# Slot list spread over shared jobs, a one-hot product on GpSimd, results stored ahead of weight loads, routed jobs written out, and a reordered end in an attention and expert layer

## The reference, cut to what matters

```python
h = _layernorm(x) * (1 + cb) + sb
scores = softmax(h @ gate_weight.T)                 # 2048 rows, 8 experts
topk_w, topk_idx = top_k(scores, 2)
topk_w = topk_w / (sum(topk_w) + 1e-20)
cw = zeros((T, E)).at[arange(T)[:, None], topk_idx].add(topk_w)
g = silu(einsum('th,efh->tef', x, w_gate)) * einsum('th,efh->tef', x, w_up)    # F = 352
expert_out = einsum('tef,ehf->teh', g, w_down)
y = einsum('te,teh->th', cw, expert_out) + swiglu(x, shared weights of width 704)
x = x + gb * y
```

## Time and profile before

| what | value |
|---|---|
| median of 3 executions | 1620.08 us (1616.24, 1620.08, 1622.06) |
| profiled execution | 1621.21 us |
| its span in the trace | 1619.4 us |
| TensorE busy in the span | 1539.6 us, 95% |
| VectorE / ScalarE / GpSimd busy | 1026.9 / 727.8 / 667.8 us |
| mean granted TensorE clock | 0.98 |

### The profile page before, as it was taken

The page is one execution under the profiler, slowest core; times in us unless marked ns, Lnnn a source line. Parts: engine busy times, 40 slices in busy tenths (PEclk is TensorE's granted clock), DMA queues, the critical chain, the costliest instruction groups (busy, mean ns, idle before and its releaser), DMA issues.

```text
span 1619.4 us, 29774 instructions
## 1 busy us (share of the span) xinstructions
PE 1539.6 (95%) x8844; PEld 1364.3 (84%) x8845; DVE 1026.9 (63%) x2255; ACT 727.8 (45%) x1728; POOL 667.8 (41%) x713
## 2 busy tenths in 40 slices
PE   6899999997999999999999999979999899999997
PEld 3677778886999999999999999868988788888896
DVE  5966666665777777777777777876576222222267
ACT  3542222345666666666666666522231232233232
POOL 2113333345666665656666666525212111111053
PEclk9999999997999999999999999989998999999999
DMA  7335555576748475757665666274131455755465
GB/s 257 137 130 180 204 202 199 191 258 215 240 148 252 144 240 165 241 172 220 191 202 184 210 182 215 102 265 173 63 115 55 171 180 204 264 194 196 173 199 172
DMA packets 203231, 303.81 MB, mean 188 GB/s; under 512 B 80337, under 2 KB 142161, under 8 KB 196001
## 3 DMA queue, kind: packets, MB, share of 16 engines
q1 hardware_dynamic: 193312, 276.82, 50.7%
q0 software_dynamic: 5680, 18.62, 4.0%
q10 hardware_dynamic: 4176, 7.60, 1.4%
HBM read 187.35 MB, written 115.64 MB: 187 GB/s over the span
## 4 chain that ended last, share of the span: by engine, by line
PE 77%; DVE 9%; DMA 8%; issue 3%; ACT 2%; POOL 1%; SPq 0%; ACTq 0%; DVEq 0%; POOLq 0%
PE bank L1405 40%; PE bank L1500 15%; PE bank L1613 7%; PE bank L1565 7%; DMA slot_results<-y_sb 6%; PE bank L1596 4%; PE bank L1662 1%; PE bank L1418 1%; PE bank L1698 1%; DMA keys<-k_ring 1%; DVE ht_lo L2184 1%; DVE h L2162 1%; DVE h L2165 1%; DMA xin<-ffn_rows,slot_tokens 1%; ACT prob L1235 0%
## 5 line engine op out<-in xcount | busy, mean ns | idle before, releaser
L1405 PE MATMUL bank<-w,xt_hi 128*128 (+2 forms) x1136 | 286.3, 334 | 7.5 <-issue 4.6
L1405 PEld LDWEIGHTS bank<-w,xt_hi 128*128 128x128 f32 x1136 | 198.3, 191 | 19.4 <-issue 14.9
L1405 PE MATMUL bank<-w,xt_lo 128*128 (+2 forms) x568 | 185.3, 326 | 0.0
L1247 ACT ACTIVATE prob<-prob,row_inv 128x128 f32<-128x128 f32 (+3 forms) x256 | 137.2, 560 | 82.0 <-DVE row_inv L2056 81.8
L2184 DVE TENSOR_TENSOR ht_lo<-bank,ht_hi 128x128 fp32r<-128x128 f32 (+1 forms) x213 | 48.3, 282 | 195.1 <-ACT ht_hi L1342 194.9
L1405 PE MATMUL bank<-w,ht_hi 128*128 (+3 forms) x426 | 143.4, 418 | 23.3 <-DVE ht_lo L2184 23.3
L1235 ACT ACTIVATE prob<-bank,neg_max 128x128 f32<-128x128 f32 (+3 forms) x256 | 133.8, 526 | 49.0 <-DVE neg_max L2048 48.8
L1405 PE MATMUL bank<-wv_hi,h_hi 128*128 128x256 f32 x512 | 148.5, 290 | 0.0
L1405 PE MATMUL bank<-wv_lo,h_hi 128*128 128x256 f32 x512 | 145.7, 285 | 0.0
L1405 PE MATMUL bank<-wv_hi,h_lo 128*128 128x256 f32 x512 | 145.7, 285 | 0.0
L900 POOL CAST q_hi<-q_raw 128x512 fp32r<-128x512 f32 x64 | 71.5, 1118 | 137.7 <-PE bank L1565 117.1
(11 more groups left out here) (227 smaller groups left out, 4101.0 us busy)
## 6 DMA issues: line engine op xcount, KB each, us to landing
keys<-k_ring SPq DMA_DIRECT2D x64, 512.0 KB, 3.0
ch_raw<-wexp SPq DMA_DIRECT2D x128, 170.0 KB, 3.1
experts_hi<-ch_hi SPq DMA_DIRECT2D x128, 170.0 KB, 2.6
experts_lo<-ch_lo SPq DMA_DIRECT2D x128, 170.0 KB, 2.7
w<-experts_hi SPq DMA_DIRECT2D x10, 2176.0 KB, 8.9
w<-experts_lo SPq DMA_DIRECT2D x10, 2176.0 KB, 15.3
q_transposed<-q_out SPq DMA_DIRECT2D x64, 256.0 KB, 2.0
k_even<-keys SPq DMA_DIRECT2D x16, 1024.0 KB, 5.5
```

Of the source, the lines that this page charges most:

```text
L1247: ins = act.activation(part, part, ACT.Copy, scale=row_inv[:, h, r:r + 1])
L1405: ins = pe.matmul(dst, a, m, start=(k == 0), stop=(k == last))
```

## The change

- **Slot list.** The routing work of VectorE is dealt out differently: `slots_of` and both `position` calls run inside job 17, the one-hots of c = 0 inside job 18 and those of c = 1 inside job 19 (both `lanes` of a c together), the copy of the slot list and `begun` inside job 20, `halves` behind it, and `table` inside job 21. TensorE's two `slot_tokens` move from the ends of jobs 18 and 19 into jobs 19 and 20, between the up product and the transposes of the next rows.
- **A product on GpSimd.** `tile_hot` = `tile_eq` times `token` moves from VectorE to GpSimd, ahead of `add_shared(17)` and `add_shared(18)`.
- **GpSimd order.** `gather_x(2)` goes ahead of `add_shared(20)` and `add_shared(21)`, and for every later slot `gather_x(r + 1)` goes ahead of `weights_ready(r)`.
- **Stores first.** SyncE stores the result of slot r-1 ahead of the weight loads of step r, not behind them.
- **Routed jobs written out.** On TensorE all 39 slots stand one after the other without a loop, and the offset of the next slot is read once, ahead of `down`.
- **The end.** The last addition to `acc` of six tiles (`by_pool`: places 0, 2, 4, 6, 8, 10 of `GATHER`) moves from VectorE to GpSimd, which makes it ahead of the gathers that reuse the buffer. In the last job VectorE combines tile 15 and adds it to `acc` ahead of the last `ht_part`, then finishes tile 14 while TensorE makes the last product, and then adds the last bank times `gb` to tile 15.

```diff
--- before
+++ after
@@ -74,7 +74,12 @@
-TOKENS_AT = [NT + 2, NT + 3]
+def by_pool(i):
+    return i % 2 == 0 and i < NT - TT
+TOKENS_AT = [NT + 3, NT + 4]
@@ -570,6 +575,11 @@
+        def finished(i):
+            return ((f_pool, i // 2 + 1) if by_pool(i) else
+                    (f_ok, len([k for k in range(i + 1) if not by_pool(k)])))
@@ -828,6 +838,8 @@
                 n = r + R0
                 nxt = sp.value_load(tab[0:1, 3, bass.ds(r, 1)], min_val=1, max_val=E + 1)
                 load = [sp.value_load(tab[0:1, 4 + s, bass.ds(r, 1)], min_val=0, max_val=1) for s in range(2)]
+                if not (isinstance(r, int) and r == 0):
+                    store_y(r - 1, (k + 1) % 2)
                 wait_apart(sp, (y_full, n))
@@ -835,8 +847,6 @@
                           .then_inc(w_ld[s], 16)
-                if not (isinstance(r, int) and r == 0):
-                    store_y(r - 1, (k + 1) % 2)
@@ -852,7 +862,7 @@
             for i, t in enumerate(GATHER):
-                sp.wait_ge(f_ok, i + 1)
+                sp.wait_ge(*finished(i))
                 sp.dma_start(out_t[:, t, :], acc[:, t, :]).then_inc(out_st, 16)
@@ -1042,8 +1052,16 @@
-            for n in range(NT + 1, NT + 3):
-                add_shared(n)
+            def tile_match(c):
+                pool.wait_ge(tile_eq_ok, c + 1)
+                pool.tensor_tensor(tile_hot[:, c, :, :], tile_eq[:, c, :, :],
+                                   cf("token", NT).unsqueeze(2).to_broadcast([P, NT, NOH]),
+                                   ALU.mult).then_inc(tile_hot_ok, 1)
+            for c in range(2):
+                tile_match(c)
+                add_shared(NT + 1 + c)
@@ -1073,20 +1091,29 @@
             weights_ready(1)
+            gather_x(2)
             add_shared(R0 - 2)
             add_shared(R0 - 1)
-            gather_x(2)
             for r in range(2, NSLOT):
-                weights_ready(r)
                 if r + 1 < NSLOT:
                     gather_x(r + 1)
+                weights_ready(r)
+            def add_tile(i):
+                pool.wait_ge(f_gb, i + 1)
+                a = acc[:, GATHER[i], :]
+                pool.tensor_tensor(a, a, h2[:, i % TT, :], ALU.add).then_inc(f_pool, 1)
...
                 if i >= TT:
-                    pool.wait_ge(f_ok, i - TT + 1)
+                    if by_pool(i - TT):
+                        add_tile(i - TT)
+                    pool.wait_ge(*finished(i - TT))
                 for c, rows in enumerate((xr, h2)):
@@ -1708,15 +1735,19 @@
             def job(n, s, wofs, prev_ofs, route=False, prev=True, nxt=True, free=None, up_ld=None, prev_at=WD,
-                    gathered=False):
+                    gathered=False, amid=None, ahead=None):
                 half(n, s, wofs, 0, route)
...
                 half(n, s, wofs, 1, route)
+                if amid:
+                    amid()
                 if nxt:
                     turn_rows(n + 1, 1 - s, loaded(n + 1, 1 - s, gathered))
+                if ahead:
+                    ahead()
                 if prev:
@@ -1758,9 +1789,8 @@
             for n in range(NT + 1, R0):
-                job(n, n % 2, W1, W1, free=(y_gb, n - 2))
-                if n in TOKENS_AT:
-                    slot_tokens(TOKENS_AT.index(n))
+                job(n, n % 2, W1, W1, free=(y_gb, n - 2),
+                    amid=(lambda: slot_tokens(TOKENS_AT.index(n))) if n in TOKENS_AT else None)
@@ -1770,30 +1800,19 @@
-            def routed(j):
-                for k in range(2):
-                    r = j * 2 + k
-                    n = r + R0
-                    if k == 1:
-                        was = at
-                    at = offset(r)
-                    if isinstance(j, int) and j == 0:
-                        prev_ofs, free = W1 if k == 0 else was, (y_gb, n - 2)
-                    else:
-                        prev_ofs = was if k == 1 else offset(r - 1)
-                        free = (y_gb, R0) if isinstance(j, int) and j == 1 and k == 0 else (y_ev, r - 2)
-                    pe.wait_ge(w_ready, r + 1)
-                    job(n, k, at, prev_ofs, free=free, gathered=True)
-            routed(0)
-            routed(1)
-            with pe.Fori(2, NSLOT // 2) as j:
-                routed(j)
-            r = NSLOT - 1
-            pe.wait_ge(w_ready, r + 1)
-            job(r + R0, 0, offset(r), offset(r - 1), free=(y_ev, r - 2))
+            at = [offset(0)]
+            def next_offset(r):
+                if r < NSLOT:
+                    at.append(offset(r))
+            for r in range(NSLOT):
+                n = r + R0
+                pe.wait_ge(w_ready, r + 1)
+                job(n, r % 2, at[r], at[r - 1] if r else W1, free=(y_gb, n - 2) if r < 3 else (y_ev, r - 2),
+                    gathered=r + 1 < NSLOT, ahead=lambda: next_offset(r + 1))
             pe.wait_ge(w_ld[0], 32 * (E // 2 + 1))
-            job(Z0, 1, 0, offset(r), free=(y_ev, NSLOT - 2))
+            job(Z0, 1, 0, at[NSLOT - 1], free=(y_ev, NSLOT - 2))
             for n in range(Z0 + 1, NJ):
@@ -2348,12 +2366,10 @@
-                link(dve.tensor_tensor(tile_eq[:, c, :, :],
-                                       cf("slot_tile", NOH).unsqueeze(1).to_broadcast([P, NT, NOH]),
-                                       pos_f[:, c, 1, :].unsqueeze(2).to_broadcast([P, NT, NOH]), ALU.is_equal))
-                dve.tensor_tensor(tile_hot[:, c, :, :], tile_eq[:, c, :, :],
-                                  cf("token", NT).unsqueeze(2).to_broadcast([P, NT, NOH]),
-                                  ALU.mult).then_inc(tile_hot_ok, 1)
+                dve.tensor_tensor(tile_eq[:, c, :, :],
+                                  cf("slot_tile", NOH).unsqueeze(1).to_broadcast([P, NT, NOH]),
+                                  pos_f[:, c, 1, :].unsqueeze(2).to_broadcast([P, NT, NOH]),
+                                  ALU.is_equal).then_inc(tile_eq_ok, 1)
@@ -2411,24 +2427,31 @@
             first_tiles()
-            shared_job(NT + 1, slots_of)
-            position(0)
-            position(1)
+            def positions():
+                slots_of()
+                position(0)
+                position(1)
+            def one_hots(c):
+                if c == 0:
+                    dve.wait_ge(x1_ok, B)
+                    dve.wait_ge(h2_st, 16 * B + 32)
+                tile_match(c)
+                lanes(c, 0)
+                lanes(c, 1)
+            def tokens():
+                slot_tokens()
+                begun()
+            shared_job(NT + 1, positions)
             parts(0)
             parts(1)
-            dve.wait_ge(x1_ok, B)
-            dve.wait_ge(h2_st, 16 * B + 32)
-            tile_match(0)
-            lanes(0, 0)
-            shared_job(NT + 2, lambda: lanes(0, 1))
-            tile_match(1)
-            lanes(1, 0)
-            shared_job(NT + 3, lambda: lanes(1, 1))
-            begun()
-            slot_tokens()
-            shared_job(NT + 4, halves)
-            table()
-            shared_job(NT + 5)
+            shared_job(NT + 2, lambda: one_hots(0))
+            shared_job(NT + 3, lambda: one_hots(1))
+            shared_job(NT + 4, tokens)
+            halves()
+            shared_job(NT + 5, table)
             weights()
@@ -2459,8 +2485,9 @@
                 dve.tensor_tensor(a, a, mods[:, t // TT, 3, :], ALU.mult).then_inc(f_gb, 1)
-                dve.wait_ge(f_gb, i + 1)
-                dve.tensor_tensor(acc[:, t, :], acc[:, t, :], a, ALU.add).then_inc(f_ok, 1)
+                if not by_pool(i):
+                    dve.wait_ge(f_gb, i + 1)
+                    dve.tensor_tensor(acc[:, t, :], acc[:, t, :], a, ALU.add).then_inc(f_ok, 1)
@@ -2468,18 +2495,24 @@
-            for n in range(Z0, NJ):
+            for n in range(Z0, NJ - 1):
                 k = n - Z0
-                job(n, n % 2, "routed", n + 1 < NJ)
+                job(n, n % 2, "routed", True)
                 if k >= 2:
                     both(2 * k - 4)
-                    if k == NB2 - 1:
-                        combine(2 * k - 3)
-                    else:
-                        both(2 * k - 3)
+                    both(2 * k - 3)
+            job(NJ - 1, (NJ - 1) % 2, "routed", False)
+            a, gb = h2[:, (NT - 1) % TT, :], mods[:, B - 1, 3, :]
+            combine(NT - 1)
+            link(dve.tensor_tensor(a, a, gb, ALU.mult))
+            link(dve.tensor_tensor(acc[:, NT - 1, :], acc[:, NT - 1, :], a, ALU.add))
             ht_part(NJ - 1)
-            add_last(NT - 1)
-            finish_tile(NT - 1)
+            both(NT - 2)
+            dve.wait_ge(y_full, NJ)
+            link(dve.tensor_tensor(a, bank[4 + (NJ - 1) % 2][:, :], gb, ALU.mult))
+            dve.tensor_tensor(acc[:, NT - 1, :], acc[:, NT - 1, :], a, ALU.add).then_inc(f_ok, 1)
```

More of the change, by code:

```diff
@@ L476, in adaln_layer @@
         c_stat = sem("c_stat")
-        g_hi_ok = sem("g_hi_ok")
         h2_ok = sem("h2_ok")
@@ L515, in adaln_layer @@
         f_w2 = sem("f_w2")
```

(10 more changed lines are left out.)

## The result

| | before | after |
|---|---|---|
| median | 1619.65 us (1616.24 to 1622.06, 4 executions) | 1592.15 us (1589.26 to 1593.91, 4 executions) |
| profiled execution | 1621.21 us | 1593.91 us |
| span | 1619.4 us | 1592.0 us |
| mean granted clock | 0.98 | 0.988 |

The ratio is 0.9827, with a 95% interval from 0.9806 to 0.9847: 27.5 us faster. I had predicted 1593.

What follows compares the result with a forecast made beforehand. TensorE, busy 95% of the span, was taken as the bound, leaving only gaps and lower-clock time to win. From 1621.2 us, -8.0 + 6.3 - 8.6 - 15.0 + 1.0 - 3.6 = -27.9 gave 1593.3, forecast 1593, range 1586 to 1604.

Steps and rivals of the forecast that it cites:

- Slot list, -8.0: Jobs 18 to 21: TensorE's 3.25 us gap for `ht_lo` shrinks to 0.4 and the lower clock goes, gaining 8.0 us.
- Product on GpSimd, at nothing: Job 18: the `tile_hot` product moved to GpSimd takes 1.6 us, waits for one `lane_hot`, and adds nothing to the sum.
- My bound of 2.2 for its duration: GpSimd's product was to take 1.6 to 2.2 us; at 2.2 it would be 0.1 late for `slot_tokens(0)`.
- Table, +6.3: Start of job 22: the later `table` delays `w_ready`, a new 4.1 us gap plus 2.2 for the clock, losing 6.3 us.
- The price of the clock, 2.2: Behind the new gap at the table: lower clock costs between 0 and 5.2 us, taken as 2.2.
- Gather, -8.6: Job 23 to 24: `gather_x(2)` issued before the weight load removes TensorE's 6.39 us wait and its clock loss, gaining 8.6 us.
- 0 to 1 us to spare: `gather_x(3)`, in the old place behind the load, just fits; if it doesn't, the gather gain is 7.6 us.
- Slots, -15.0: Jobs 24 to 58: stores first and jobs written out regain 15.0 of 15.4 us lost, bounds 4.5 and 15.4.
- the loop was not the cost: Rival on the slots: offsets and register addresses cost the same in straight code, 10.5 us stay, 1604 us; chance 0.12.
- Additions on GpSimd, +1.0: Last shared jobs: six additions leave VectorE, but GpSimd's SBUF additions slow its steps; a loss of 1.0 us, between -1.7 and +3.
- The end, -3.6: Last job: last product starts 2.0 us earlier and runs 1.5 shorter, later links save 0.1; gain 3.6, or 1.9 us.
- Ahead of 1200 us, at nothing: Before 1200 us: only one rewritten wait between two VectorE steps on the gate columns, costed at nothing.

Runs made afterwards that it cites:

- before, stores first: The kernel before with each result store moved ahead of the weight loads, slots still in a loop: median 1609.82 us, ratio to before 0.9931.
- before, slots written out: The kernel before with only TensorE's routed slots written out straight and the offset read once: median 1624.83 us, ratio to before 1.0016.

## Why the prediction was right, and where not

**Slot list, -8.0: right, 7.5.** The gap went as walked, to 0.64 and not to 0.4. A cast in `parts` took 1.16 us at 1217.13, where the other casts take 0.18, since it ran beside GpSimd's addition (1216.96 to 1218.25, where the cast ends at 1218.29). These 0.98 us are more than the whole gap of 0.64: without them I would expect none. No run undid this edit alone. Of the 7.5 us, 2.6 are the gap and 4.9 the clock behind it, and the latter is not fixed: in "before, stores first" the same gap cost 3.2 us less, and against that profile the edit would have been worth 4.3.

**Product on GpSimd, at nothing: right.** My bound of 2.2 for its duration was broken, by a mechanism that I had named for the additions and not carried over far enough. The first product took 3.32 us and began inside the pair of `lane_hot`: from the pair's end at 1223.68 to its own at 1224.81 are 1.1 us. The second took 2.18 us, and there one of the two `lane_hot` took 2.29 where the earlier trace rows has 1.22. So the product itself is an estimated 1.1 us, and it waits for one or two `lane_hot`, or they for it. TensorE came 1.3 us later still (1226.1), so the cover of a microsecond held.

**Table, +6.3: the gap right in kind, both sizes too large.** 3.02 for 4.1, of which 1.0 is the table itself: its nine steps took 2.0 us, while my 3.0 came from the earlier trace rows, in which one step had run beside GpSimd. The price of the clock, 2.2, was 0 in this execution and in four others with the same gap, and 1.5 and 2.5 in two. So 2.2 lies in the range and is too large on average, 0.6 over the seven. Of the 3.5 us, 0.5 lie in the two jobs beside the gap and are not named by any wait. So -1.1 in the gap, -2.2 in the clock and +0.5 make the -2.8 by which this term was over.

**Gather, -8.6: right to 0.1,** alone (15.34 to 6.72) and in the whole. `gather_x(3)` had "0 to 1 us to spare": 24 to 25 took 7.16, 0.4 more than 6.72, and in two later profiles of nine the gather was late and the step took 8.35 and 8.48.

**Slots, -15.0: the total right (14.6), the split wrong.** This is the step of the prediction that failed. I split 15.4 us into 4.5 for stores, 4.6 for turns and the rest, as shares that add, each read from TensorE's own list of waits. They don't add. Stores first alone gave 9.2, straight jobs alone nothing (a loss of 2.6 in the profile), the two together 15.1. A store that lands late holds ScalarE for up to 5.2 us, and the time that TensorE loses at its turns meanwhile makes its wait shorter; so what TensorE waits for by name, 4.5 us, was the part the turns didn't cover. I also left out that a longer wait can bring the lower clock, 1.3 to 1.6 us each time in the two straight kernels with late stores. My rival "the loop was not the cost" was not true either: with the stores out of the way the turns cost 5.9. The sum held because the change made both edits. Had only the straight code been changed, the same working would have promised 10 us for none. On this the Trainium skill's page "Runtime: NRT & Kernel Launch" (section "Instruction fetch mechanics") was right in that straight code cost nothing more, 6.72 us for each of 33 jobs. That a taken branch costs something fits the 0.35 us a turn, though the second offset read at the turn is in it too.

**Additions on GpSimd, +1.0: somewhat low, 1.9 in the marks, 1.7 to 2.2 by the experiment.** Beside GpSimd's 1.31 an addition of VectorE took 2.02, which is 0.69 + 1.31, so it waited for the whole of the other. The Trainium skill's page "SBUF — State Buffer" (section "Who interferes with whom") has this exclusion, and these rows agree. The 3.4 us that I worked out by it were too much; that TensorE's pace hid the rest was not tested. The edit was a small loss.

**The end, -3.6: right, 4.0,** and 3.6 by experiment. A product start 1.7 us earlier (3.35 to 1.64) and a product at the full clock, 2.34 us in place of 3.82, 1.5 us. I had 2.0 and 1.5, and 0.1 for the last links; 0.9 came ahead of and behind the product. VectorE's steps of tile 14 now end 0.4 us behind the product, so an even faster product would have given nothing.

**Ahead of 1200 us, at nothing: +1.9.** All of it lies ahead of job 1, whose mark stands at 1085.63 before and 1087.57 after; from there to job 16 both took 113.5 us. Nothing of the change lies there, and the stretch moves from execution to execution: in three profiles of after the mark stands at 1087.57, 1084.31 and 1081.08. The jobs from 1 to 16 took between 113.1 and 118.3 us over all the profiles as well. The sum had no term for any of this, and it happened to cancel against the table.

The forecast's 1593 therefore came out close in part by luck, because terms were off by up to 2.8 us in opposite directions. Measured less predicted, they are -2.8 at the table, +1.9 ahead of job 1, +0.9 at the additions, and about half a microsecond or less elsewhere. The median was to stand 1.1 us under the profiled execution, so the sum as written gives 1592.2, which I had put at 1593. The mechanisms of the other terms held; the largest term, the slots, had the right total and the wrong working.

## What to carry to other kernels

- A wait that TensorE's list names is only what is left after its other delays have covered the rest. Before splitting a loss into shares, ask which delay hides which. The pair that interacts should be tried alone, both ways.
- Put short transfers ahead of long ones in one queue if both are due together: one store moved ahead of the load was worth 9.2 us with four lines of text.
- A transfer with no time to spare is late in some executions only. The gather of slot 3 was on time in seven profiles and late in two, and one profile of each kernel would have blamed an edit. Compare its issue time with its neighbours' before naming a cause, and move it if that is cheap.
- Before an edit is credited with a stretch, look at the clock in it. The same gap of 3.2 us in job 18 cost 3.2 us less in one profile than in another.

## What the runs showed of the hardware that was not expected

- A gap of 3.02 us at the same place left the granted clock at 1.00 in five profiles and gave 0.50 behind it in two. The price was 0 in the five, 1.5 and 2.5 us in the two. In "before, slots written out" gaps of 2.08 and 2.58 us were followed by 0.50 and one of 3.02 was not. So here the length of a gap alone did not decide.
- A product of 128x640 on GpSimd took 3.32 us when VectorE's pair of `lane_hot` was under way and 2.18 the second time, when one `lane_hot` took 2.29 in place of 1.22. And a VectorE cast of 128x32 took 1.16 us in place of 0.18 while GpSimd added, and ended within 0.04 us of it.
- A wait for a releaser called remote, 3.9 to 5.4 us on ScalarE, stands in job 63 of all twelve later profiles, and with it one of 2.3 to 3.9 on VectorE in eleven. Its cause was not found, and nothing was tried against it.
